# State output of the tower phase in two matmul passes instead of three, and a 64-column second pass on the state input

## The reference

```
def ssm(x, a_diag, Bm, Cm, Dm):
    a = jax.nn.sigmoid(a_diag)
    u = jnp.einsum('btd,ds->bts', x, Bm)
    def step(h, u_t):
        h = a * h + u_t
        return (h, h)
    h0 = jnp.zeros((x.shape[0], a.shape[0]), x.dtype)
    _, H = jax.lax.scan(step, h0, jnp.swapaxes(u, 0, 1))
    H = jnp.swapaxes(H, 0, 1)
    return jnp.einsum('bts,sd->btd', H, Cm) + jnp.einsum('btd,de->bte', x, Dm)
...
for l in range(L):
    x = x + ssm(layernorm(x, ln1_s[l], ln1_b[l]), A_diag[l], B[l], C[l], D[l])
    h = layernorm(x, ln2_s[l], ln2_b[l])
    h = jax.nn.gelu(jnp.einsum('btd,df->btf', h, w1[l]) + b1[l], approximate=False)
    x = x + jnp.einsum('btf,fd->btd', h, w2[l]) + b2[l]
```

## Time and profile before

| | |
|---|---|
| median of 3 runs | 1409.2 us (1407.94 to 1412.7) |
| the profiled execution's own time | 1410.45 us |
| its span, first to last instruction | 1408.7 us |
| tower phase, about | 0 to 551 us of the span |
| PE busy over the whole span | 1255.0 us, 89% |
| mean granted TensorE clock | 0.968 |

### The profile page before, as it was taken

One profiled execution on the slowest core, in us unless ns is written; L12 is line 12 of the kernel. 1 busy time (PEld: TensorE's weight loads), 2 busy tenths in 40 slices (PEclk: granted clock), 3 DMA queues, 4 the chain that ended last, 5 costly groups with the idle time before them and its releaser, 6 DMA issues. The chain is left out here.

```text
span 1408.7 us, 26506 instructions
## 1 busy us (share of the span) xinstructions
PE 1255.0 (89%) x9120; PEld 1074.1 (76%) x9120; DVE 1017.0 (72%) x2691; ACT 917.4 (65%) x2009; POOL 565.4 (40%) x601
## 2 busy tenths in 40 slices
PE   0699999999999994899947788999999999999986
PEld 0599888889998994677635566888888887888886
DVE  2666666666667646998747787888888888888744
ACT  1554665674575643998816776778777788777743
POOL 5512351341344213454414565435544445444320
PEclk9899999999999997999968999999999999999999
DMA  8200010010000001000040002000100000000000
GB/s 193 66 1 1 14 61 1 14 61 1 1 1 1 1 0 53 2 17 17 16 113 1 2 5 84 5 5 5 44 4 3 20 5 12 20 20 21 20 30 16
DMA packets 43568, 33.74 MB, mean 24 GB/s; under 512 B 20092, under 2 KB 40112, under 8 KB 43440
## 3 DMA queue, kind: packets, MB, share of 16 engines
q1 hardware_dynamic: 32272, 29.12, 6.6%
q0 software_dynamic: 768, 2.10, 0.8%
q10 hardware_dynamic: 10400, 0.82, 0.6%
HBM read 25.75 MB, written 4.19 MB: 21 GB/s over the span
## 5 line engine op out<-in xcount | busy, mean ns | idle before, releaser
L324 ACT ACTIVATE t_gf<-t_ps_f,t_fb_cur 128x512 f32<-128x512 f32 x128 | 88.1, 688 | 175.5 <-PE t_ps_f L248 173.2
L462 DVE TENSOR_TENSOR t_g_lo<-t_gf,t_g_hi 128x512 fp32r<-128x512 f32 x128 | 90.7, 710 | 89.3 <-ACT t_g_hi L326 88.4
L261 PE MATMUL t_ps_o<-t_w_hi,t_g_hi 128*128 128x256 f32 x512 | 145.3, 284 | 0.0
L262 PE MATMUL t_ps_o<-t_w_lo,t_g_hi 128*128 128x256 f32 x512 | 143.9, 281 | 0.0
L263 PE MATMUL t_ps_o<-t_w_hi,t_g_lo 128*128 128x256 f32 x512 | 143.4, 280 | 0.0
L1587 PE MATMUL w_ring<-w_nh,w_w_hi 128*128 128x256 f32 x384 | 114.0, 297 | 12.9 <-DVE w_nl L2102 5.5
L561 POOL TENSOR_TENSOR t_rs<-t_ve,t_neghalf 128x4 f32<-128x4 f32 x32 | 37.4, 1170 | 195.6 <-DVE t_ve L423 193.8
L2272 POOL TENSOR_TENSOR w_m<-w_m 128x512 f32<-128x512 f32 x64 | 85.4, 1335 | 67.7 <-DVE w_m L2019 67.6
L246 PE MATMUL t_ps_f<-t_nh,t_w_hi 128*128 128x512 f32 x256 | 104.2, 407 | 8.6 <-DVE t_nl L438 4.7
L1589 PE MATMUL w_ring<-w_nl,w_w_hi 128*128 128x256 f32 x384 | 109.5, 285 | 0.0
L1588 PE MATMUL w_ring<-w_nh,w_w_lo 128*128 128x256 f32 x384 | 109.5, 285 | 0.0
(11 more groups left out here) (266 smaller groups left out, 4369.2 us busy)
## 6 DMA issues: line engine op xcount, KB each, us to landing
t_raw<-in_L_tok_w SPq DMA_DIRECT2D x8, 1024.0 KB, 5.2
out<-X SPq DMA_DIRECT2D x14, 256.0 KB, 2.1
raw<-in_L_ffn_wqkv SPq DMA_DIRECT2D x2, 1536.0 KB, 7.4
raw<-in_L_ffn_w SPq DMA_DIRECT2D x4, 682.0 KB, 6.3
w_raw_o<-out SPq DMA_DIRECT2D x8, 256.0 KB, 2.7
w_xs<-X SPq DMA_DIRECT2D x16, 127.0 KB
w_raw<-in_L_ffn_w SPq DMA_DIRECT2D x2, 640.0 KB
t_raw_d<-in_L_tok_D SPq DMA_DIRECT2D x4, 256.0 KB
```

The source lines that it names most:

```text
L261: pe.matmul(out, g_hi[:, j % 4, tok], w2_hi[:, j, :], start=(j == 0 and t % 2 == 0), stop=False, skip_group_check=True)
L262: pe.matmul(out, g_hi[:, j % 4, tok], w2_lo[:, j, :], start=False, stop=False, skip_group_check=True)
L324: act.activation(gf[:, j % 2, :], ps_f[:, j % 2, :], ACT.Gelu, bias=fb_cur[:, j:j + 1]).then_inc(pf_free, 1)
L462: dve.tensor_tensor(g_lo[:, j % 4, :], gf[:, j % 2, :], g_hi[:, j % 4, :].bitcast(F32), ALU.subtract).then_inc(g_split, 1)
```

## The change

`state_out` now does two passes for C in place of three. The first is as before: `hs_hi` by `c_hi`, over all 128 partitions. For the second a new operand `hs_cat` holds in partitions 0 to 63 the rounded states once more, and in partitions 64 to 127 the low part of those same states; its partner `c_cat` holds low C in the lower partitions and C rounded in the upper ones. One pass then adds both missing products for partitions 0 to 63 of the state. Both missing products of the upper 64 partitions (the states of the low part of B) are dropped: they are low by low.

For this ScalarE issues one more activation of 64x512 after `state_hi` (semaphore `hs_twin`, on which PE waits too); VectorE's subtraction covers 64 partitions and writes to the other half; `front_parts` has a multiplication by a 0/1 mask `top` in place of the copy to `b_hiz`. `b_hiz` is gone: the low pass of `state_in` takes the 64 high columns of `b_cat` and writes 64 partitions.

```
             for c in range(DC):
-                pe.matmul(ps_u[:, 0, :], b_cat[:, c, :], nh[0][:, c, :], start=(c == 0), stop=False)
-                mm = pe.matmul(ps_u[:, 0, :], b_hiz[:, c, :], nl[0][:, c, :], start=False, stop=(c == DC - 1))
+                pe.matmul(ps_u[:, 0, :], b_cat[:, c, :], nh[0][:, c, :], start=(c == 0), stop=False, skip_group_check=True)
+                mm = pe.matmul(ps_u[0:S, 0, :], b_cat[:, c, 0:S], nl[0][:, c, :], start=False, stop=(c == DC - 1), skip_group_check=True)
...
             pe.wait_ge(hs_split, n + 1)
+            pe.wait_ge(hs_twin, n + 1)
...
-                passes += [(hs_hi[:, tok], c_hi[:, :]), (hs_hi[:, tok], c_lo[:, :]), (hs_lo[:, tok], c_hi[:, :])]
+                passes += [(hs_hi[:, tok], c_hi[:, :]), (hs_cat[:, tok], c_cat[:, :])]
...
             act.activation(hs_hi[:, :], hs[:, :], ACT.Copy).then_inc(hs_hi_done, 1)
+            act.activation(hs_cat[0:S, :], hs[0:S, :], ACT.Copy).then_inc(hs_twin, 1)
...
-            dve.tensor_tensor(hs_lo[:, :], hs[:, :], hs_hi[:, :].bitcast(F32), ALU.subtract).then_inc(hs_split, 1)
+            dve.tensor_tensor(hs_cat[S:2 * S, :], hs[0:S, :], hs_hi[0:S, :].bitcast(F32), ALU.subtract).then_inc(hs_split, 1)
...
         eng.tensor_copy(b_cat[:, :, 0:S], raw_b[:, :, :])
-        eng.tensor_copy(b_hiz[:, :, 0:S], raw_b[:, :, :])
         eng.tensor_copy(c_hi[:, :], raw_c[:, :])
+        eng.tensor_tensor(c_top[:, :], raw_c[:, :], top[:, :], ALU.mult)
...
-        eng.tensor_tensor(c_lo[:, :], raw_c[:, :], c_hi[:, :].bitcast(F32), ALU.subtract)
+        eng.tensor_tensor(c_cat[:, :], raw_c[:, :], c_top[:, :].bitcast(F32), ALU.subtract)
...
-        dve.memset(b_hiz[:, :, :].bitcast(F32), 0.0).then_inc(s_keep, 1)
+        dve.memset(top[0:S, :], 1.0)
+        dve.memset(top[S:2 * S, :], 0.0).then_inc(s_keep, 1)
```

More of the change, by code:

```diff
@@ L71, in tower_phase @@
         b_cat = sb("b_cat", [P, DC, 2 * S], F32R)
-        b_hiz = sb("b_hiz", [P, DC, 2 * S], F32R)
         c_hi = sb("c_hi", [P, D], F32R)
-        c_lo = sb("c_lo", [P, D], F32R)
+        c_top = sb("c_top", [P, D], F32R)
+        c_cat = sb("c_cat", [P, D], F32R)
+        top = sb("top", [P, D])
         d_hi = sb("d_hi", [P, DC, D], F32R)
@@ L109, in tower_phase @@
         hs_hi = sb("hs_hi", [P, GTOK], F32R)
-        hs_lo = sb("hs_lo", [P, GTOK], F32R)
+        hs_cat = sb("hs_cat", [P, GTOK], F32R)
         gf = sb("gf", [P, 2, GTOK])
@@ L139, in tower_phase @@
         pf_free = sem("pf_free")
-        u_full, scanned, hs_hi_done, hs_split = sem("u_full"), sem("scanned"), sem("hs_hi_done"), sem("hs_split")
+        u_full, scanned, hs_hi_done, hs_twin, hs_split = sem("u_full"), sem("scanned"), sem("hs_hi_done"), sem("hs_twin"), sem("hs_split")
         y_full, f_full = sem("y_full"), sem("f_full")
```

## The result

| | before | changed |
|---|---|---|
| median of 6 runs, us | 1412.62 (1407.94 to 1413.0) | 1403.36 (1401.2 to 1405.91) |
| ratio, with 95% interval | | 0.9943 (0.9928 to 0.9957) |
| profiled execution, own time, us | 1410.45 | 1405.06 |
| its span, us | 1408.7 | 1403.1 |
| PE busy, us | 1255.0 | 1250.7 |

The change made the kernel faster by 0.57%, some 8 us by this ratio (the two medians alone lie 9.3 us apart), with both ends of the interval beyond 0.3%. I had forecast no change (+0.5 us). The number 1403.36 lies inside the range of 1401.5 to 1414.0, but at its faster rival (1401.7), not at its forecast (1409.7).

The account below looks back on a forecast made before the run. PE's stream was taken to bound the kernel. Twelve plain fronts (+0.8 us), three in a layer's last step (-0.3) and the first (0) made +0.5 on the median 1409.2, so 1409.7 us, range 1401.5 to 1414.0.

Parts of the forecast that it names:

- faster rival: In state_in, tile changes around the lone 64-column pass are free and the state_out wait stays: 1401.7 us; chance 0.17.
- What bounds the tower: Tower phase: PE's stream sets the pace, busy 118.4 of 120 us, so a dropped pass counts almost one to one.
- The pass that goes: In state_out, four passes of 256 columns fewer in each of 16 fronts: 0.47 us less per front, 7.5 us in all.
- The tile changes: In state_in, two entries at 0.15 us and two exits at 0.20 us around the 64-column passes: 0.70 us more per front.
- The wait that should go: At the start of state_out, 0.16 us per plain front and 0.34 in a layer's last step no longer lost.
- ScalarE and POOL: In the fronts, ScalarE's added activation (0.64 us at most) and POOL's mask multiplication (0.74 us) are covered and cost nothing.
- The slower rival of half pace: In state_in, each 64-column low pass takes 0.43 us instead of 0.23: 6.4 us more, 1416; chance 0.08.
- The dearer drain: In state_in, tile changes after a long pass expose 0.16 us instead of 0.10: 3.8 us more, 1413.5; chance 0.05.

Follow-up runs that it names:

- e7_fp32_tile_at_0: Changed kernel with the low pass of state_in as plain fp32 instead of fp32r, still one 128*64 tile at column 0; 1431.94 us.
- e8_fp32_full: Changed kernel with the low pass of state_in as plain fp32 on the full 128*128 tile; no total time given, 0.86 us per fp32 pass of 512 columns.
- e4_fp32_pair: Changed kernel with the low pass of state_in as two plain fp32 128*64 tiles side by side; 1433.47 us.
- e9_late_wait: Changed kernel with PE waiting for the split states only ahead of the first tile's two C passes, after its six D passes; 1396.32 us, ratio to before 0.9895.
- e1_two_passes_full_low: Changed kernel with the low pass of state_in on 128 columns again, two-pass state_out kept; 1404.22 us, ratio to before 0.9946.

## Why the prediction was wrong

*What bounds the tower.* Right: every PE pass that went came back whole, 0.49 us per plain step for 0.47.

*The pass that goes.* Right: 7.5 us forecast, ratio 0.9946 with this part alone, which is 7.6 us of 1411 (0.9927 to 0.9964: 5 to 10 us).

*The tile changes.* **This step failed**: "So the tile costs it, not the type. Per front: 2 x 0.15 + 2 x 0.20 = 0.70 us more." Measured: 0. The size was right for what the earlier trace rows show, fp32 on 128*64, as `e7_fp32_tile_at_0` reproduces to 0.01 us. The control in the earlier trace rows showed that the type alone costs nothing, which `e8_fp32_full` confirms, and I took from it that the tile alone costs. It did not follow: that control had neither the narrow tile nor fp32r on one. What costs is an fp32 tile or a row tile; an fp32r pass on fewer columns is free. The Trainium skill (TensorEngine Tiling (Array Packing), Key Properties) says that a change of mode drains TensorE. The traces have a loss at each change for 64*128 in fp32r (0.78 us for four) and for 128*64 in fp32 (0.70 us), and none for 128*64 or 128*32 in fp32r (0.23 us from start to start), so where the rule applies can't be read off the tile size that the profile prints.

*The wait that should go.* It stayed, 0.49 us where 0.51 had been, because it was to be paid by PE's coming 0.20 us later after the last tile change. Without that price there was nothing to pay it. The reasoning itself holds: in `e7_fp32_tile_at_0`, where each change costs, the distance is 0.35 us and nothing is lost. It counted 0.12 us for the weight load, the distance of the passes, where the earlier trace rows print a length of 0.19; that nothing was lost speaks for the smaller number. This miss follows from the same error as the one above.

*ScalarE and POOL.* Right: the second copy (0.61 us) ended before VectorE's subtraction, and POOL's multiplication by the mask cost nothing that a plain step shows.

*The rivals.* The faster one, with the tile changes free and the wait in place, said 1401.7 from a base of 1409.2, 7.5 us less; measured are 8 us less. That the measured time lies in the stated range is owed to this rival, for whose sake the range reached so low, and not to the sum. I gave it 0.17, since "no row shows a lone 128*64 pass" stood against two places that both showed a loss. Both places were the same kind of pass, so they were one piece of evidence. The slower rival of half pace is refuted by the changed kernel's own timeline (0.22 and 0.24 us behind L221, where it asked for over 0.37); `e8_fp32_full` and `e4_fp32_pair` show that the third phase's slower pace is that of plain fp32. The dearer drain did not come up: the price in `e7_fp32_tile_at_0` is the one of the short passes.

## What to carry to other kernels

A price read from another phase holds for the passes that it was read from: before it is carried over, list all in which they differ (type, tile, position, company), and see whether a control varies them together, not one by one. Where PE is the bound, a dropped pass pays in full, and a wait belongs right ahead of the first pass that needs it, here behind the six passes that do not: that was worth some 4 us on the kernel before and 7 on the changed one, of which the traces account for 4. It stops paying when another engine is last: behind 24 passes in place of six it brought nothing more. The combination `e9_late_wait` stands at 0.9895 of before.

## What the runs showed of the hardware

- fp32r with 64 or 32 stationary columns at column 0 costs nothing between full passes: 0.23 us for 512 columns on both sides, though the profile prints 128*64 or 128*32. Plain fp32 on 128*64 costs 0.70 us for two entries and two exits, at column 0 or 64, alone or in a pair; fp32r on 64*128 costs 0.78.
- A plain fp32 pass of 512 columns takes 0.86 us in two records, an fp32r one 0.23; the change of type alone costs nothing. Two fp32 tiles side by side take the time of one.
- Behind a layer's end, where PE stands idle for 1.5 to 2.1 us, a stretch of 3.4 us at half clock (512 columns in 0.43 us) shows in six of thirteen traces and costs about 1.6 us; the length of the idle time alone does not decide it (2.06 us before without such a stretch, 1.79 in `e1_two_passes_full_low` with one). This is as large as a fifth of the effect under study, so single spans don't tell it.
